# Rounding to fp4 in the last stage of a transformer layer: the power of two from two bits, the clamp inside the addition, and the scales of x and h together

## The chip, the cores and the metric

The kernel runs on one core of one Trainium2 chip. The core has a matrix engine (TensorE, PE in the rows), a vector engine (VectorE, DVE), a scalar engine (ScalarE, ACT), a general engine (GpSimd, POOL) and a queue for transfers (SyncE, SP). They run side by side and wait for each other on semaphores. The metric is the device time of one execution in microseconds (us); lower is better. The profile is one execution on the chip, and its times count from the start of its span.

## The reference

The layer takes x of 4 x 2048 tokens with 256 channels. In short:

```python
x = layernorm(x + attention(x))        # 16 heads of 16, rotary positions, softmax
x = layernorm(x + ffn(x))

def fp4_quant_dequant(x):              # blocks of 16 along the last dimension
    scale = max(max(abs(block)) / 6, 1e-12)
    xn = block / scale                 # so |xn| <= 6
    idx = searchsorted([0.25, 0.75, 1.25, 1.75, 2.5, 3.5, 5.0], abs(xn))
    return [0, .5, 1, 1.5, 2, 3, 4, 6][idx] * sign(xn) * scale

def fp4_linear(x, w): return fp4_quant_dequant(x) @ fp4_quant_dequant(w).T
def ffn(x):                            # 256 -> 704 -> 256
    h = silu(fp4_linear(x, w_gate)) * fp4_linear(x, w_up)
    return fp4_linear(h, w_down)
```

The grid has steps of 0.5 below 2, of 1 from 2 to 4 and of 2 above 4. The step follows from the power of two p = 1, 2 or 4 at or below |xn| (1 for everything smaller). Adding p * 1.5 * 2^22 to xn in float32 and subtracting it again rounds xn to the grid.

## The kernel before

Three stages follow each other: projections and rotary positions (to about 310 us), attention (to about 3115 us), and the last stage, which this document is about (about 3115 us to the end). The last stage goes over 64 tiles of 128 tokens. On each engine one list of functions says what is done in step s, each entry with a lag: an entry (6, f) runs f on tile s - 6. `run_steps` writes this list out for the first and last steps, and between them makes a loop (`Fori`) whose body holds four steps, with semaphore values computed from a register; `run_straight` writes all steps out with constants. The order within a step is the order of the list, and every engine works its instructions strictly in that order.

What a step s does on each engine, in order, with the tile in brackets:

- **VectorE**: every fourth step the small arithmetic of the inverse deviations, `inverse_std` (L988 to L993), in front; then `residual2` [s-10] (L1007, L1009), `residual1` [s-2] (L1000, L1002); every fourth step `variance` (L961 to L969); then `quantise_xh`: x of tile s-6 and h of tile s-8 in one hand-written interleaving of eight operations each (k = 1 to 8, lines L853 to L868); then `silu_up` [s-7] (L1037).
- **GpSimd**: `normalise` [s-1] (L1124, L1125), `round_x` [s-6] and `round_h` [s-8] in two halves, each a subtraction (L1130) and a multiplication by the scale (L1132). In the order of time, `normalise` stands ahead of `round_x` of the same step, that is, right behind `round_h` of the step before.
- **TensorE**: transposes of x [s-7] (L657), `proj` [s-2] (L649), `gate_up` [s-7] (L679), transposes of h [s-9] (L670), `down` [s-9] (L689).
- **ScalarE**: copy of the transposed x [s-7] (L803), `norm2` [s-14] (L793), `norm1` [s-6] (L787), the store, every fourth step a square root (L827) with two table loads, `silu` [s-7] (L820), copies of the transposed h [s-9] (L810, L813).

Three buffer waits matter. `residual2` of tile n waits for `norm2` of tile n-4, whose row it overwrites (`o_done`). `residual1` of tile n waits for `norm1` of tile n-4 (`x1_done`). `norm1` waits for `residual2` of the same step (`y2_done`). The eight operations of the rounding on VectorE are, for x (256 columns, 16 blocks) and for h (704 columns, 44 blocks): k=1 largest magnitude of each block, k=2 the inverse scale's base, k=3 the scale, k=4 reciprocal, k=5 values times the inverse, k=6 the exponent bits (an AND with 0x7F800000), k=7 the power of two clamped from below at 1 and times 1.5 * 2^22, k=8 the sum. k=6 and k=7 read one tensor and constants; k=5 and k=8 read two tensors in SBUF.

Of the kernel before, what the change touches and what calls it, by code (L numbers as in the profile page):

```python
# [22 lines left out]
I32 = mybir.dt.int32  # L23
ALU = mybir.AluOpType
ACT = mybir.ActivationFunctionType
AX = mybir.AxisListType

P = 128
# [32 lines left out]
ROUND = 1.5 * 2.0 ** 22  # L61
EXPONENT = 0x7F800000
TILES_S = KT * CHUNKS
PAIRS = TILES_S // 2
# [58 lines left out]
def run_steps(eng, total, stages):  # L123


    longest = max(lag for lag, _ in stages)

    first = -(-(longest + UNROLL) // UNROLL) * UNROLL
    last = total // UNROLL * UNROLL

    def straight(s):
        for lag, fn in stages:
            if 0 <= s - lag < total:
                fn(At(0, s - lag))

    if last - first < UNROLL:
        first = last = total + longest
    for s in range(first):
        straight(s)
    if last > first:  # L140
        with eng.Fori(0, (last - first) // UNROLL) as register:
            i = Turn(eng, register)
            for u in range(UNROLL):
                for lag, fn in stages:
                    fn(At(i, first + u - lag))
        for s in range(last, total + longest):
            straight(s)

# [32 lines left out]
def layer_kernel(nc, x, xT, sinT, cosT, w_qk, w_v, b_qk, b_v, w_proj, b_proj, w_gate, w_up, w_down, eye, out):  # L181
    nc.disable_value_cache = True
    ctx = ExitStack()
    with ctx:
# [3 lines left out]
        def sem(name):  # L188
            return ctx.enter_context(nc.semaphore(name))
# [96 lines left out]
        std, rstd, shift, ln_t, ln_d, sums, var = (take(8) for _ in range(7))  # L286
        x_am, x_sc, x_inv = ([take(C // BLK) for _ in range(2)] for _ in range(3))
        h_am, h_sc, h_inv = ([take(FF // BLK) for _ in range(2)] for _ in range(3))
        hh_r = [v_all[:, i * FF:(i + 1) * FF] for i in range(4)]
# [33 lines left out]
        var_step, std_done, ln_step, x1_done = (sem(n) for n in ("var_step", "std_done", "ln_step", "x1_done"))  # L323
        xq_step, xr_step, xh_done, xhT_psum, xhT_out = (sem(n) for n in ("xq_step", "xr_step", "xh_done", "xhT_psum", "xhT_out"))
        gu_psum, e_done, h_done = (sem(n) for n in ("gu_psum", "e_done", "h_done"))
# [13 lines left out]
        def _(sp):  # L339
# [121 lines left out]
            def load_tile(b, q, c):  # L461

                if not isinstance(q, int):
# [15 lines left out]
            for p in range(4):  # L479
                sp.wait_ge(inv_out[p], 16 * G // 4)  # L480
            with sp.Fori(1, KT // 4) as q:
                for c in range(4):
                    load_tile(0, q, c)
            with sp.Fori(1, B) as b:
                with sp.Fori(0, KT // 4) as q:
                    for c in range(4):
                        load_tile(b, q, c)


        @block.tensor  # L490
        def _(pe):
# [200 lines left out]

            run_steps(pe, TILES, [(7, xT_tile), (2, proj), (7, gate_up), (9, hT_tile), (9, down)])


        @block.scalar
        def _(act):
# [125 lines left out]
            def deviation(n, alone):  # L823
# [4 lines left out]

            run_steps(act, TILES, [
                (7, xT_out), (14, norm2), (6, norm1), (14, store_out),  # L830
# [6 lines left out]
        def _(dve):  # L837
            def quantise(jobs):
# [4 lines left out]
                def bc(a, blocks):  # L843
                    return a.unsqueeze(2).broadcast_to([P, blocks, BLK])
                order = [(0, k) for k in range(1, 9)]
                if len(jobs) > 1:
                    order = [(int(o[0] == "b"), int(o[1])) for o in "a1 b1 a2 a3 b2 a4 b3 a5 b4 a6 b5 a7 a8 b6 b7 b8".split()]
                for j, k in order:
                    for x, xn, m, am, sc, inv, step, at, blocks in jobs[j:j + 1]:
                        if k > 1:  # L850
# [159 lines left out]

            def job_x(n):
                p = n.u % 2
# [3 lines left out]
                return (x1_r[n.u], xh_r[n.u], xm_r[p], x_am[p], x_sc[p], x_inv[p], xq_step, lambda k: n.times(8, k), C // BLK)  # L1016

            def job_h(n):
                p = n.u % 2
                wait_after(dve, hq_done, n.times(2, -2))  # L1020
                dve.wait_ge(h_done, n.times(2, 2))
                return (hh_r[n.u], hh_r[n.u], hm_r[p], h_am[p], h_sc[p], h_inv[p], hq_step, lambda k: n.times(8, k), FF // BLK)

            def quantise_xh(n):

                quantise([job_x(n)] + ([job_h(n.back(2))] if n.c >= 2 else []))

            def quantise_last_h(n):
                if n.static(TILES - 2) or n.static(TILES - 1):
                    quantise([job_h(n)])  # L1030

            def silu_up(n):
# [6 lines left out]

            run_steps(dve, TILES, [  # L1040
                (3, lambda n: inverse_std(n, False)), (11, lambda n: inverse_std(n, True)),
# [5 lines left out]
        def _(pool):  # L1047
# [79 lines left out]
            def rounded(t, m, sc, step, at, done, blocks):  # L1127

                v = t.rearrange("p (b e) -> p b e", e=BLK)
                nc.gpsimd.tensor_tensor(t, t, m, ALU.subtract).then_inc(step, 1)  # L1130
                pool.wait_ge(step, at)
                nc.gpsimd.tensor_tensor(v, v, sc.unsqueeze(2).broadcast_to([P, blocks, BLK]), ALU.mult).then_inc(done, 1)  # L1132

            def round_x(n):
                pool.wait_ge(xq_step, n.times(8, 8))
                rounded(xh_r[n.u], xm_r[n.u % 2], x_sc[n.u % 2], xr_step, n.times(1, 1), xh_done, C // BLK)

            def round_h(n):
                p, nb = n.u % 2, FH // BLK
                for hf in range(2):  # L1140
                    cols = slice(hf * FH, (hf + 1) * FH)
                    pool.wait_ge(hq_step, n.times(8, 8))
                    rounded(hh_r[n.u][:, cols], hm_r[p][:, cols], h_sc[p][:, hf * nb:(hf + 1) * nb], hr_step,
                            n.times(2, hf + 1), hq_done, nb)

            run_steps(pool, TILES, [(1, normalise), (6, round_x), (8, round_h)])


# [38 lines left out]
```

## Time and profile before

| | us |
|---|---|
| median of 3 runs (lowest to highest) | 3878.07 (3875.76 to 3878.23) |
| the profiled execution's own time | 3876.52 |
| its span | 3874.7 |
| TensorE busy over the span | 3617.4 (93%) |
| VectorE busy over the span | 3350.5 (86%) |
| GpSimd busy over the span | 712.0 (18%) |

Some 1.8 us of the execution lie outside the span. The times in the rows are start and duration; `DVE`, `POOL`, `ACT` are the engines, `L868` is a line of the kernel before, `x1` the number of instructions in a row, and the square bracket at the end of a row is the time that the engine stood idle before it, with whom it waited for.

### The profile page before, as it was taken

The numbers are of one execution on the slowest core, as the hardware profiler recorded it, in microseconds if no ns is written. First come the engines' busy times: TensorE is split into PE (matmuls) and PEld (weight loads), VectorE is DVE, ScalarE is ACT, GpSimd is POOL, SyncE is SP. The second block draws the span as 40 slices with busy tenths as digits, with TensorE's granted clock in tenths as the row PEclk, the third lists the DMA queues.
The fourth block names the chain that finished last, engine by engine and source line by source line (L and its number), as shares of the span: only waits on it lengthen the run. The fifth ranks groups of instructions, "written<-read, shape, count | busy, mean of one in ns | idle before, by whom it ended". The sixth has DMA issues, their size and how long they took to land.

```text
span 3874.7 us, 56176 instructions
## 1 busy us (share of the span) xinstructions
PE 3617.4 (93%) x19560; PEld 1556.6 (40%) x19560; DVE 3350.5 (86%) x3879; ACT 2527.9 (65%) x4870; POOL 712.0 (18%) x883
## 2 busy tenths in 40 slices
PE   7769999999999999999999999999999978888887
PEld 4433333333333333333333333333333346656665
DVE  7998888888888888888888888888888379999997
ACT  4334777777777777777777777777777723333333
POOL 6870000000000000000000000000000045555554
PEclk9887999999999999999999999999999989999999
DMA  5441111111111111111111111111111111111110
GB/s 153 161 167 53 44 39 38 44 45 40 37 43 45 41 37 42 46 42 37 40 47 42 38 39 48 42 38 38 46 44 39 29 50 45 43 47 45 47 37 20
DMA packets 121153, 195.55 MB, mean 50 GB/s; under 512 B 28640, under 2 KB 83040, under 8 KB 108640
## 3 DMA queue, kind: packets, MB, share of 16 engines
q1 hardware_dynamic: 111712, 184.16, 14.2%
q10 hardware_dynamic: 9216, 8.39, 0.6%
q8 instruction: 140, 2.29, 0.2%
q14 instruction: 85, 0.70, 0.1%
HBM read 139.55 MB, written 51.38 MB: 49 GB/s over the span
## 4 chain that ended last, share of the span: by engine, by line
PE 70%; issue 10%; POOL 8%; DVE 7%; ACT 3%; DMA 1%; POOLq 0%; SPq 0%; ACTq 0%; DVEq 0%
PE ps L563 28%; PE ps L605 26%; PE ps L594 14%; POOL v_all L1130 2%; ACT arena L772 2%; DVE arena L904 2%; DVE arena L909 1%; POOL arena L1130 1%; POOL arena L1132 1%; POOL arena L1124 1%; POOL arena L1125 1%; DVE arena L927 1%; PE ps L679 1%; DVE arena L897 1%; POOL arena L1065 1%
## 5 line engine op out<-in xcount | busy, mean ns | idle before, releaser
L927 DVE TENSOR_REDUCE arena<-ps 128x1 f32<-128x1024 f32 x2048 | 2412.7, 1220 | 332.8 <-PE ps L563 326.5
L772 ACT ACTIVATE arena<-ps 128x512 f32<-128x512 f32 x4096 | 2122.0, 604 | 622.5 <-PE ps L594 622.4
L594 PE MATMUL ps<-qst,kst 51*128 51x512 f32 x4096 | 1529.7, 453 | 31.1 <-ACT arena L772 7.7
L563 PE MATMUL ps<-kst,qst 48*128 48x512 f32 x4096 | 1284.4, 433 | 27.5 <-DMA qst<-qk_parts 23.2
L605 PE MATMUL ps<-arena 128*32 128x512 f32 x8192 | 1092.5, 605 | 2.4
L563 PEld LDWEIGHTS ps<-kst,qst 48*128 48x128 f32 x4096 | 622.8, 187 | 1090.0 <-DVE arena L927 942.9
L594 PEld LDWEIGHTS ps<-qst,kst 51*128 51x128 f32 x4096 | 677.3, 184 | 493.6 <-ACT arena L772 491.5
L1107 POOL TENSOR_TENSOR arena<-arena,ones 128x16 bf16<-128x16 f32 x64 | 14.2, 222 | 2640.5 <-DVE arena L932 2640.5
L605 PEld LDWEIGHTS ps<-arena 128*32 128x32 f32 x8192 | 163.0, 108 | 245.3 <-ACT arena L772 148.9
L689 PE MATMUL ps<-wdT,arena 128*128 128x256 f32 (+1 forms) x768 | 191.0, 400 | 36.1 <-ACT arena L810 36.1
L679 PE MATMUL ps<-wgT,arena 128*128 128x352 f32 x512 | 202.3, 478 | 3.5 <-DVE v_all L1037 2.5
L679 PE MATMUL ps<-wuT,arena 128*128 128x352 f32 x512 | 198.6, 470 | 0.0
L803 ACT ACTIVATE arena<-ps 128x256 f32<-128x256 f32 x64 | 24.5, 383 | 247.3 <-PE ps L657 247.3
L689 PEld LDWEIGHTS ps<-wdT,arena 128*128 128x128 f32 (+1 forms) x768 | 146.0, 197 | 69.9 <-ACT arena L810 42.0
L820 ACT ACTIVATE v_all<-ps 128x352 f32<-128x352 f32 x128 | 56.6, 462 | 122.8 <-PE ps L679 121.4
L1130 POOL TENSOR_TENSOR v_all<-v_all 128x352 f32<-128x352 f32 x128 | 119.3, 932 | 60.4 <-DVE v_all L868 60.4
L536 PE MATMUL ps<-arena 128*128 128x512 f32 x256 | 117.5, 613 | 12.6 <-DMA arena<-in_b_qk 9.4
L679 PEld LDWEIGHTS ps<-wuT,arena 128*128 128x128 f32 x512 | 100.5, 196 | 57.7 <-issue 6.2
L679 PEld LDWEIGHTS ps<-wgT,arena 128*128 128x128 f32 x512 | 97.7, 198 | 56.9 <-ACT arena L803 6.8
L735 ACT ACTIVATE arena<-ps,arena 128x512 f32<-128x512 f32 x64 | 41.2, 700 | 116.2 <-DMA qk_parts<-arena 105.2
L543 PE MATMUL ps<-arena 128*128 128x256 f32 x256 | 69.5, 432 | 40.5 <-ACT v_all L726 40.5
L1130 POOL TENSOR_TENSOR arena<-arena 128x256 f32<-128x256 f32 x64 | 59.7, 932 | 254.0 <-DVE arena L868 254.0
(101 smaller groups left out, 2282.7 us busy)
## 6 DMA issues: line engine op xcount, KB each, us to landing
qk_parts<-arena SPq DMA_DIRECT2D x32, 1024.0 KB, 7.4
kst<-qk_parts SPq DMA_DIRECT2D x128, 256.0 KB
qst<-qk_parts SPq DMA_DIRECT2D x128, 256.0 KB
kst<-qk_parts SPq DMA_DIRECT2D x128, 128.0 KB
qst<-qk_parts SPq DMA_DIRECT2D x128, 128.0 KB
att<-arena SPq DMA_DIRECT2D x256, 34.0 KB
arena<-in_xT SPq DMA_DIRECT2D x16, 512.0 KB, 8.2
arena<-att SPq DMA_DIRECT2D x128, 64.0 KB
```

What stands on the lines that cost most here:

```text
L536: mm = nc.tensor.matmul(ps[:, m, :], wqk[:, c, m * P:(m + 1) * P], xt[p][:, c], start=(c == 0), stop=(c == CT - 1))
L543: mm = nc.tensor.matmul(ps[:, 4 + v, t * C:(t + 1) * C], xt[p][:, c, (2 * v + t) * P:(2 * v + t + 1) * P], wv[:, c], start=(c == 0), stop= ...
L563: mm = nc.tensor.matmul(ps[:, i % S_BANKS, :], q[SROW:SROW + STACK, qt * P:(qt + 1) * P], k[SROW:SROW + STACK, kc * CHUNK:(kc + 1) * CHUNK ...
L594: nc.tensor.matmul(ps[:, t_bank(t_place(g.c, i)), :], kst[g.u % 2][0:ROWS, kb * P:(kb + 1) * P], qst[g.u % 2][0:ROWS, qb * CHUNK:(qb + 1) ...
L605: mm = nc.tensor.matmul(ps[32 * qb:32 * qb + 32, O_BANK, :], vs[g.u % 2][:, kb, :], pt[kb % 2][:, qb * CHUNK:(qb + 1) * CHUNK], start=(kb ...
L679: mm = nc.tensor.matmul(ps[:, bank, 0:FH], xhT_r[n.u % 2][:, ct], w[:, ct, hf * FH:(hf + 1) * FH], start=(ct == 0), stop=(ct == CT - 1))
L689: mm = nc.tensor.matmul(ps[:, 7, 0:C], hT_r[n.u % 2][0:nf, j], wdT[0:nf, k], start=(j == 0), stop=(j == 5))
L772: nc.scalar.activation(pt[kb % 2][:, qb * CHUNK:(qb + 1) * CHUNK], ps[:, t_bank(t_place(g.c, i)), :], ACT.Exp).then_inc(p_ready, 1)
L820: nc.scalar.activation(e_r[n.u % 2][:, hf * FH:(hf + 1) * FH], ps[:, 2 + 2 * hf, 0:FH], ACT.Silu).then_inc(e_done, 1)
L904: nc.vector.tensor_tensor(x, x, rot[p], ALU.add).then_inc(qr_done, 1)
L927: nc.vector.tensor_reduce(mx[g.u % 2][:, i // 2, i % 2:i % 2 + 1], ps[:, bank:bank + 2, :].rearrange("p b t -> p (b t)"), AX.X, ALU.max).t ...
L1130: nc.gpsimd.tensor_tensor(t, t, m, ALU.subtract).then_inc(step, 1)
```

## The change

In the last stage only. The rounding takes the power of two and its product with 1.5 * 2^22 in one integer operation: an AND with 0x40800000 leaves the exponent's top and lowest bits, and an XOR with 0x0B400000 makes from them exactly 4 or 2 times 1.5 * 2^22 where |xn| is 4 or 2 and more, and a tiny number otherwise. The clamp (a maximum with 1.5 * 2^22) is then taken inside the addition, as a three-input operation (`scalar_tensor_tensor`, max and add). The tile m therefore no longer holds the clamped number that GpSimd subtracts, so GpSimd takes the same maximum on its own copy first: one `tensor_scalar` more in front of each of its three subtractions per tile. The base of the inverse, the scale and the reciprocal are computed once for the 16 blocks of x and the 44 of h side by side (60 numbers). Loops become straight code on all five engines (`run_steps` goes; SP's `Fori` loops over the tile loads too).

```diff
+POWER_BITS, TO_ROUND = 0x40800000, 0x0B400000
...
+            def scales(p, cols, turn):
+                nc.vector.tensor_scalar(q_inv[p][:, cols], q_am[p][:, cols], BELOW / 6.0, 1e-12 * BELOW, ALU.mult, ALU.max
+                                        ).then_inc(q_small, 1)
+                nc.vector.tensor_scalar(q_sc[p][:, cols], q_am[p][:, cols], 1.0 / 6.0, 1e-12, ALU.mult, ALU.max
+                                        ).then_inc(q_small, 1)
+                dve.wait_ge(q_small, turn.times(3, 1))
+                nc.vector.reciprocal(q_inv[p][:, cols], q_inv[p][:, cols]).then_inc(q_small, 1)
+                dve.wait_ge(q_small, turn.times(3, 3))
...
+            def powers_x(n):
+                dve.wait_ge(x_scaled, n.times(1, 1))
+                nc.vector.tensor_scalar(xm_r[n.u % 2].bitcast(I32), xh_r[n.u].bitcast(I32), POWER_BITS, TO_ROUND,
+                                        ALU.bitwise_and, ALU.bitwise_xor).then_inc(x_power, 1)
+            def round_x(n):
+                dve.wait_ge(x_power, n.times(1, 1))
+                nc.vector.scalar_tensor_tensor(out=xh_r[n.u], in0=xm_r[n.u % 2], scalar=ROUND, in1=xh_r[n.u],
+                                               op0=ALU.max, op1=ALU.add).then_inc(xq_step, 1)
...
             def quantise_xh(n):
-                quantise([job_x(n)] + ([job_h(n.back(2))] if n.c >= 2 else []))
+                p, h = n.u % 2, n.back(2)
+                largest_x(n)
...
+                largest_h(h)
+                dve.wait_ge(q_max, n.times(2, 0))
+                scales(p, slice(0, HB.stop), n)
+                scale_x(n)
+                scale_h(h)
+                powers_x(n)
+                round_x(n)
+                powers_h(h)
+                round_h(h)
...
             def rounded(t, m, sc, step, at, done, blocks):
                 v = t.rearrange("p (b e) -> p b e", e=BLK)
+                nc.gpsimd.tensor_scalar(m, m, ROUND, None, ALU.max).then_inc(step, 1)
+                pool.wait_ge(step, at[0])
                 nc.gpsimd.tensor_tensor(t, t, m, ALU.subtract).then_inc(step, 1)
-                pool.wait_ge(step, at)
+                pool.wait_ge(step, at[1])
                 nc.gpsimd.tensor_tensor(v, v, sc.unsqueeze(2).broadcast_to([P, blocks, BLK]), ALU.mult).then_inc(done, 1)
...
-            run_steps(pool, TILES, [(1, normalise), (6, round_x), (8, round_h)])
+            run_straight(TILES, [(1, normalise), (6, round_x), (8, round_h)])
```

## Rows read from the trace of the kernel before

**Rows 1.** Busy time of the engines in a stretch of 100 us of the last stage:

```profile
core 0: us, PE busy (x) PEld busy (x) DVE busy (x) ACT busy (x) POOL busy (x), PEclk, DMA share, GB/s
3400.00:3500.00 100.00, 85.38 (x353) 60.16 (x352) 92.15 (x218) 32.40 (x66) 56.57 (x70) 0.98 0.17 47
```

**Rows 2.** VectorE in order of time, one step without small arithmetic:

```profile
3394.87 0.43 DVE L868 TENSOR_TENSOR arena<-arena 128x256 f32<-128x256 f32 x1
...
3395.77 0.93 DVE L866 TENSOR_SCALAR v_all<-v_all 128x704 f32<-128x704 f32 x1
3396.73 1.19 DVE L868 TENSOR_TENSOR v_all<-v_all 128x704 f32<-128x704 f32 x1
...
3398.85 0.42 DVE L1007 TENSOR_TENSOR arena<-ps,arena 128x256 f32<-128x256 f32 x1
...
3400.89 0.42 DVE L853 TENSOR_REDUCE arena<-arena 128x16 f32<-128x256 f32 x1
...
3402.25 0.71 DVE L855 TENSOR_SCALAR arena<-arena 128x44 f32<-128x44 f32 x1
...
3405.10 0.42 DVE L868 TENSOR_TENSOR arena<-arena 128x256 f32<-128x256 f32 x1
```

**Rows 3.** GpSimd in order of time in the same step:

```profile
3395.38 0.94 POOL L1130 TENSOR_TENSOR arena<-arena 128x256 f32<-128x256 f32 x1 [5.54 <-DVE arena L868]
3396.39 0.78 POOL L1132 TENSOR_TENSOR arena<-arena 128x256 f32<-128x256 f32 x1
...
3401.51 0.72 POOL L1124 TENSOR_TENSOR arena<-arena 128x256 f32<-128x256 f32 x1
```

**Rows 4.** ScalarE in order of time in the same step:

```profile
3398.23 0.59 ACT L793 ACTIVATE arena<-arena 128x256 f32<-128x256 f32 x1
```

**Rows 5.** VectorE, the rounding of a step in which GpSimd was done:

```profile
3437.09 0.42 DVE L853 TENSOR_REDUCE arena<-arena 128x16 f32<-128x256 f32 x1
...
3438.37 0.18 DVE L855 TENSOR_SCALAR arena<-arena 128x44 f32<-128x44 f32 x1
...
3439.09 0.42 DVE L859 RECIPROCAL arena<-arena 128x44 f32<-128x44 f32 x1
...
3439.57 0.88 DVE L861 TENSOR_TENSOR v_all<-v_all,arena 128x704 f32<-128x704 f32 x1
...
3440.68 0.43 DVE L868 TENSOR_TENSOR arena<-arena 128x256 f32<-128x256 f32 x1
```

**Rows 6.** VectorE, the two steps with small arithmetic:

```profile
3415.35 0.43 DVE L868 TENSOR_TENSOR arena<-arena 128x256 f32<-128x256 f32 x1
...
3427.58 0.43 DVE L868 TENSOR_TENSOR arena<-arena 128x256 f32<-128x256 f32 x1
...
3431.43 0.18 DVE L988 RECIPROCAL arena<-arena 128x8 f32<-128x8 f32 x1
...
3435.05 0.42 DVE L1007 TENSOR_TENSOR arena<-ps,arena 128x256 f32<-128x256 f32 x1 [0.75 <-ACT arena L793]
```

**Rows 7.** GpSimd's groups by line and shape, whole span (count, busy us, mean ns):

```profile
L1130 POOL TENSOR_TENSOR v_all<-v_all 128x352 f32<-128x352 f32 x128 | 119.3, 932 | 60.4 <-DVE v_all L868 60.4
L1132 POOL TENSOR_TENSOR v_all<-v_all,arena 128x352 f32<-128x352 f32 x128 | 100.8, 788 | 10.0
...
L1100 POOL COPY arena<-v_all 128x256 f32<-128x256 f32 x64 | 25.4, 396 | 0.0
...
L1091 POOL MEMSET arena<- 128x240 f32 x2 | 0.6, 302 | 0.0
```

**Rows 8.** First stage, in order of time: VectorE beside GpSimd, then GpSimd alone:

```profile
110.68 2.28 DVE L897 TENSOR_TENSOR arena<-arena 128x2048 f32<-128x2048 f32 x1
...
110.84 6.51 POOL L1071 TENSOR_TENSOR arena<-arena 128x2048 f32<-128x2048 f32 x1 [1.16 <-DVE arena L909]
...
274.11 4.51 POOL L1071 TENSOR_TENSOR arena<-arena 128x2048 f32<-128x2048 f32 x1 [3.49 <-DVE arena L909]
```

**Rows 9.** VectorE, the same operation four steps apart in steps written out straight:

```profile
3189.73 0.41 DVE L1007 TENSOR_TENSOR arena<-ps,arena 128x256 f32<-128x256 f32 x1
...
3235.30 0.42 DVE L1007 TENSOR_TENSOR arena<-ps,arena 128x256 f32<-128x256 f32 x1
```

More of the change, by code:

```diff
@@ L120, in run_straight @@
                 fn(At(0, s - lag))
[L123 to L147, printed above, removed]
 def t_place(g, i):
@@ L286, in layer_kernel @@
         std, rstd, shift, ln_t, ln_d, sums, var = (take(8) for _ in range(7))
-        x_am, x_sc, x_inv = ([take(C // BLK) for _ in range(2)] for _ in range(3))
-        h_am, h_sc, h_inv = ([take(FF // BLK) for _ in range(2)] for _ in range(3))
+        XB, HB = slice(0, C // BLK), slice(C // BLK, C // BLK + FF // BLK)
+        q_am, q_sc, q_inv = ([take(HB.stop) for _ in range(2)] for _ in range(3))
         hh_r = [v_all[:, i * FF:(i + 1) * FF] for i in range(4)]
@@ L480, in _ @@
                 sp.wait_ge(inv_out[p], 16 * G // 4)
[L481 to L487, printed above, removed]
+            for tile in range(4, TILES):
+                load_tile(tile // KT, tile % KT // 4, tile % 4)
         @block.tensor
@@ L844, in bc @@
                     return a.unsqueeze(2).broadcast_to([P, blocks, BLK])
[L845 to L849, printed above, removed]
+                for k in range(1, 9):
+                    for x, xn, m, am, sc, inv, step, at, blocks in jobs:
                         if k > 1:
@@ L1009, in residual2, with blocks, over, largest_x @@
                 nc.vector.bn_stats(bn[:, 4 + n.u], y2_r[n.u]).then_inc(y2_step, 1)
-            def job_x(n):
-                p = n.u % 2
+            def blocks(a):
+                return a.rearrange("p (b e) -> p b e", e=BLK)
+            def over(small, cols):
+                return small[:, cols].unsqueeze(2).broadcast_to([P, cols.stop - cols.start, BLK])
+            def scales(p, cols, turn):
[6 more added lines that the diff above has]
+                dve.wait_ge(q_small, turn.times(3, 3))
+            def largest_x(n):
                 dve.wait_ge(x1_done, n.times(1, 1))
@@ L1015, in job_x, with largest_h @@
                 wait_after(dve, xh_done, n.times(1, -1))
-                return (x1_r[n.u], xh_r[n.u], xm_r[p], x_am[p], x_sc[p], x_inv[p], xq_step, lambda k: n.times(8, k), C // BLK)
-            def job_h(n):
-                p = n.u % 2
+                nc.vector.tensor_reduce(q_am[n.u % 2][:, XB], blocks(x1_r[n.u]), AX.X, ALU.max, apply_absolute_value=True
+                                        ).then_inc(q_max, 1)
+            def largest_h(n):
                 wait_after(dve, hq_done, n.times(2, -2))
@@ L1021, in job_h, with scale_x @@
                 dve.wait_ge(h_done, n.times(2, 2))
-                return (hh_r[n.u], hh_r[n.u], hm_r[p], h_am[p], h_sc[p], h_inv[p], hq_step, lambda k: n.times(8, k), FF // BLK)
-            def quantise_xh(n):
-                quantise([job_x(n)] + ([job_h(n.back(2))] if n.c >= 2 else []))
+                nc.vector.tensor_reduce(q_am[n.u % 2][:, HB], blocks(hh_r[n.u]), AX.X, ALU.max, apply_absolute_value=True
+                                        ).then_inc(q_max, 1)
+            def scale_x(n):
+                nc.vector.tensor_tensor(blocks(xh_r[n.u]), blocks(x1_r[n.u]), over(q_inv[n.u % 2], XB), ALU.mult
+                                        ).then_inc(x_scaled, 1)
@@ new lines, in scale_h @@
+            def scale_h(n):
+                nc.vector.tensor_tensor(blocks(hh_r[n.u]), blocks(hh_r[n.u]), over(q_inv[n.u % 2], HB), ALU.mult
+                                        ).then_inc(h_scaled, 1)
+            def powers_x(n):
+                dve.wait_ge(x_scaled, n.times(1, 1))
+                nc.vector.tensor_scalar(xm_r[n.u % 2].bitcast(I32), xh_r[n.u].bitcast(I32), POWER_BITS, TO_ROUND,
+                                        ALU.bitwise_and, ALU.bitwise_xor).then_inc(x_power, 1)
@@ new lines, in round_h @@
+            def round_h(n):
+                dve.wait_ge(h_power, n.times(1, 1))
+                nc.vector.scalar_tensor_tensor(out=hh_r[n.u], in0=hm_r[n.u % 2], scalar=ROUND, in1=hh_r[n.u],
+                                               op0=ALU.max, op1=ALU.add).then_inc(hq_step, 1)
+            def quantise_xh(n):
+                p, h = n.u % 2, n.back(2)
+                largest_x(n)
+                if n.c < 2:
+                    dve.wait_ge(q_max, n.c + 1)
+                    scales(p, XB, n)
+                    scale_x(n)
+                    powers_x(n)
+                    round_x(n)
+                    return
+                largest_h(h)
+                dve.wait_ge(q_max, n.times(2, 0))
+                scales(p, slice(0, HB.stop), n)
+                scale_x(n)
+                scale_h(h)
+                powers_x(n)
+                round_x(n)
+                powers_h(h)
+                round_h(h)
```

33 lines of the change are left out of this document (22 added, 11 removed).

## The prediction

> **What bounds the kernel now.** I read the busy time by stretches first. In the last stage VectorE is busy 92% of the time, GpSimd 57%, and TensorE runs at a granted clock of 0.98 [rows 1]. So VectorE seems the bound, and an edit that takes work off it seems a gain. The engines' instructions in order of time show more. Call t = 0 the start of the sum of x (k=8) on VectorE. From there to the next one a plain step takes 3405.10 - 3394.87 = 10.23 us [rows 2], and it is a ring through four engines. GpSimd subtracts and multiplies x until 3396.39 + 0.78 = 3397.17 (t = 2.30) [rows 3]; TensorE transposes, ScalarE copies and then runs `norm2` until 3398.82 [rows 4]; `residual2` starts on VectorE at 3398.85, the first block maximum at 3400.89, and the next k=8 at 3405.10 [rows 2]. In pieces: 2.30 + 1.68 + 2.04 + 4.21. VectorE's other work in between (h and `silu_up`) ends just as `residual2` may start, so VectorE and the ring are tied. Four steps are a period: two plain ones, one with the variances (12.23), one with the inverse deviations (3440.68 - 3427.58 = 13.10) [rows 6], 45.81 in all, and 16 periods in the stage.
>
> The second thing to see is that VectorE and GpSimd stand in each other's way. GpSimd's operation over 2048 takes 4.51 alone and 6.51 when VectorE's two-input one of 2.28 began just before it [rows 8]: it waited nearly all of it. VectorE's sum of h takes 1.19 [rows 2] where an operation of that size takes 0.88 [rows 5], because it started 0.44 before GpSimd's multiplication ended; a scale operation on 44 numbers takes 0.71 under GpSimd's `normalise` [rows 2, 3] and 0.18 without it [rows 5]. So I reckon with a lock: of such operations one runs and the other waits to its end. The Trainium skill (SBUF — State Buffer, "Who interferes with whom") says the same of the port pair that the two engines share, and that a VectorE operation with one SBUF input outside the fast modes is free of it; by that rule the reductions, `residual2` and `silu_up` never wait, and the trace agrees.
>
> **The change, part by part.** *Off VectorE:* k=7 of h (0.93 [rows 2]), k=7 of x and three small operations. The sum stays a two-tensor operation; as the kernel before has no three-input one of this size I take the price of the old sum, 0.88 free of waits. The AND with XOR costs as the AND. *On the ring, the rounding of x:* from the first maximum to the scale operation that needs both maxima 3438.37 - 3437.09 = 1.28; that operation and the wait for it 0.22; the reciprocal of 60 numbers 0.52 (0.42 for 44 [rows 5], 0.57 in proportion) and its wait 0.04; scaling x until scaling h starts 0.34; from there to k=8 now 3440.68 - 3439.57 = 1.11 [rows 5], less 0.05. That is 3.46, against 3.59 now in a step free of GpSimd and 4.21 in a plain one. *On GpSimd:* three clamps per tile. The trace has no such operation. Its nearest row is the copy, also one tensor in and one out: 0.40 for 256 columns, so about 0.50 for 352; below it lies the memset of 240 (0.30, so 0.40), above it the two-input operations, 0.72 for 256 and 0.93 for 352 [rows 3, 7]. I take the copy and keep both ends. Each clamp also adds a wait of 0.08.
>
> The Trainium skill (GPSIMD Engine Reference, section 3.1) gives 1.03 cycles per element at 1.2 GHz for a loop body of up to two operations, 0.22 us for 256 columns plus the dispatch, and its standing rule is to leave elementwise work to the vector engine. By that figure, an estimate, the clamp lies between memset and copy, and the sum below would come out some 10 us lower; no row here shows the clamp itself.
>
> *A plain step put together.* On VectorE the powers of h run from t = 0.34 to 0.86. GpSimd's clamp of x is issued at 0.51, waits for them as its subtraction does now (0.94 instead of 0.72 [rows 3]), and ends at 1.12. The sum of h waits for it and runs to 1.86. The subtraction waits for that sum and ends at 2.44, the multiplication at 3.14 instead of 2.30: 0.84 late. This is what is late next. Straight code gives back about 0.15 of the 1.68 behind it: in the steps already written out straight a period is 3235.30 - 3189.73 = 45.57 [rows 9] instead of 45.81. So `residual2` starts at 4.67 and the first maximum at 6.71; VectorE stands idle for 2 us before `residual2`, so the time saved on h buys nothing there. The scale operation would be ready at 7.99. But GpSimd goes straight from x to h: its two halves take twice 0.50 + 0.08 + 0.93 + 0.08 + 0.75 from t = 3.10, to 7.78, and the first `normalise` operation then holds the lock to 8.51. The scale operation waits for it, the reciprocal starts at 8.6, and k=8 comes 1.96 later, at 10.6. Plain step: 10.6 instead of 10.23, that is +0.35, twice in a period.
>
> *The step with the variances.* Six small operations follow `residual1`; from 6.83 on, four of them each meet one GpSimd operation (ends 6.95, 7.82, 8.51, 9.20). The first maximum comes at 9.27, k=8 at 12.75: +0.5. *The step with the inverse deviations.* Here VectorE itself leads to `norm2`, and h's saving counts: the first small operation starts at 2.65 instead of 3431.43 - 3427.58 = 3.85 [rows 6]. The seven meet two to three GpSimd operations and end at 4.95 to 5.55; `residual2` starts at 5.7 to 6.3 instead of 7.47, and k=8 comes at 11.55 to 11.8, so 11.7: -1.4.
>
> *Sum:* 0.35 + 0.35 + 0.5 - 1.4 = -0.2 us per period, times 16 = -3 us. The other edits go with it: GpSimd is then busy some 8.2 of 10.6 us and keeps up; TensorE, which needs about 9.75 us a step, only gets more idle time; SP's loads are issued on the same condition (`y_done` three tiles back) and stay ahead of `normalise`. Straight code as such has no cost that the attention stage, straight already, shows. 3876.5 - 3 = 3873.5 for an execution like the profiled one, which lies 1.5 under the median; on the median, 3875.
>
> **The rivals.** *A cheap clamp (memset's price, 0.30 and 0.40).* Everything behind it comes earlier: plain steps 10.3, the variance step 12.55, the inverse step 11.4; -1.25 per period, 3858. For it: one input, one operation. *The clamp at a two-input price (0.73, 0.93).* The multiplication of x ends at 3.47, GpSimd's halves at 8.8, and `normalise` then also blocks the scaling of h: plain steps 11.35, the others 13.4 and 11.9, +2.2 per period, 3913. This is the one that ends on the other side, slower; the clamp decides it, and the point at which it passes no change is near 0.42 for 256 columns. *The addition does not hold GpSimd up* (only the fast modes would lock): the subtraction ends at 1.84, plain steps fall to 9.95, and the period by 2.5: 3838. Against it stand rows 8, where a plain two-input operation did. *VectorE was the bound after all:* it loses about 1.6 us a step, but TensorE's 9.75 us and the ring both stand in front of that; at best as the case before.
>
> **How the numbers follow.** The forecast case (3862 to 3888) has 0.42, the cheap clamp 0.22, the dear one 0.20, no lock by the addition 0.07, and 0.09 goes to lost races for the lock on VectorE's small operations, a few tenths each, slower by 10 to 20 us. A difference under 0.2%, 7.8 us, can't be told from none. Within the forecast case I give a quarter to faster, half to the same, a quarter to slower; so faster is 0.10 + 0.20 + 0.07 = 0.37, the same 0.21 and 0.08 from the edges of the rivals = 0.29, slower the rest, 0.34. The range runs from between the cheap clamp and the lock-free case to short of the dear clamp: 3850 to 3908.
>
> **What would show it.** The clamp's own duration for 256 and 352 columns. GpSimd's multiplication of x ending at t = 3.1, its busy share rising from 57% to about 75%. A 2 us gap on VectorE before `residual2` in plain steps, put down to `norm2`, and a scale operation on 60 numbers that takes 0.6 to 0.7 instead of 0.2. Steps of 10.6, 10.6, 12.7 and 11.7. The forecast is wrong if the clamp is not near 0.4, if the three-input operation is slower than 0.88, or if the operations win or lose the lock in another order than I laid out.

## The result, and the profile after

| | before | changed | |
|---|---|---|---|
| median, us (15 runs each, same chip) | 3875.76 | 3890.89 | ratio 1.0059 [1.0044, 1.0075] |
| profiled execution, us | 3876.52 | 3889.72 | its span 3874.7 and 3887.7, +13.0 |
| VectorE busy, us | 3350.5 | 3283.4 | -67.1 |
| GpSimd busy, us | 712.0 | 927.1 | +215.1 |

The kernel became slower: by 15.1 us between the medians (0.4%), by 0.6% in the ratio, whose interval does not hold 1. Five of the changed kernel's 15 runs lie at 3910 to 3920 (last section), none of the kernel before's; the other ten have a median of 3889.9, still 14 us above before. VectorE was relieved as planned, by 67 us, and GpSimd took on three times as much. The forecast was no change, 3875 us; the measured median is 16 us above it.

First the stretch of 100 us of the last stage, busy time of the engines (answers to [rows 1]):

```profile
core 0: us, PE busy (x) PEld busy (x) DVE busy (x) ACT busy (x) POOL busy (x), PEclk, DMA share, GB/s
3400.00:3500.00 100.00, 81.24 (x339) 57.12 (x340) 79.54 (x170) 33.15 (x66) 84.99 (x95) 1.00 0.17 44
```

GpSimd went from 57 to 85%, VectorE from 92 to 80%, TensorE from 85 to 81%. No engine is full, and the step became longer: a sign that they wait for each other. The groups by line and shape show what one clamp takes (answers to [rows 7]; columns: count, busy us, mean ns, idle time before):

```profile
L1167 POOL TENSOR_SCALAR v_all<-v_all 128x352 f32<-128x352 f32 x128 | 139.0, 1086 | 3.7 <-DVE v_all L1036 3.7
...
L1167 POOL TENSOR_SCALAR arena<-arena 128x256 f32<-128x256 f32 x64 | 66.9, 1045 | 93.5 <-DVE arena L1031 93.5
```

A clamp of 352 columns takes 1.09 us: more than the subtraction of two tensors of that size, 0.93 [rows 7], and more than twice what I took from the copy. The 1.05 of a clamp of x (256 columns) contains a wait for VectorE. At the start of the stage, where VectorE has no h to work on yet, it takes 0.85:

```profile
3126.92 0.85 POOL L1167 TENSOR_SCALAR arena<-arena 128x256 f32<-128x256 f32 x1 [3.14 <-DVE arena L1031]
```

Together, 139.0 + 66.9 = 205.9 us of GpSimd's 215.1 are clamps.

VectorE in order of time, one plain step of the changed kernel (answers to [rows 2]):

```profile
3398.36 0.43 DVE L1031 SCALAR_TENSOR_TENSOR arena<-arena 128x256 f32<-128x256 f32 x1
...
3399.26 0.96 DVE L1036 SCALAR_TENSOR_TENSOR v_all<-v_all 128x704 f32<-128x704 f32 x1
...
3403.01 0.42 DVE L978 TENSOR_TENSOR arena<-ps,arena 128x256 f32<-128x256 f32 x1 [1.92 <-ACT arena L767]
...
3405.06 0.40 DVE L1002 TENSOR_REDUCE arena<-arena 128x16 f32<-128x256 f32 x1
...
3406.29 0.27 DVE L990 TENSOR_SCALAR arena<-arena 128x60 f32<-128x60 f32 x1
...
3407.58 1.42 DVE L1016 TENSOR_TENSOR v_all<-v_all,arena 128x704 f32<-128x704 f32 x1
3408.91 0.81 DVE L1021 TENSOR_SCALAR arena<-arena 128x256 int32<-128x256 int32 x1
3409.76 0.42 DVE L1031 SCALAR_TENSOR_TENSOR arena<-arena 128x256 f32<-128x256 f32 x1
```

GpSimd in the same step (answers to [rows 3]):

```profile
3398.88 1.05 POOL L1167 TENSOR_SCALAR arena<-arena 128x256 f32<-128x256 f32 x1 [1.50 <-DVE arena L1031]
3400.01 0.80 POOL L1169 TENSOR_TENSOR arena<-arena 128x256 f32<-128x256 f32 x1
...
3401.47 1.09 POOL L1167 TENSOR_SCALAR v_all<-v_all 128x352 f32<-128x352 f32 x1
...
3406.59 0.79 POOL L1171 TENSOR_TENSOR v_all<-v_all,arena 128x352 f32<-128x352 f32 x1
3407.33 0.91 POOL L1161 TENSOR_TENSOR arena<-arena 128x256 f32<-128x256 f32 x1
3408.21 1.37 POOL L1162 TENSOR_TENSOR arena<-arena,bp_bc 128x256 f32<-128x256 f32 x1
```

Read the two side by side. The step takes 3409.76 - 3398.36 = 11.40 us instead of 10.23. The 1.92 us gap on VectorE before `residual2` (L978) is the one forecast. New is the end of the step. GpSimd finishes h only at 3407.38, and `normalise` (L1161, L1162) then lies exactly over the scaling of h (L1016) and the powers of x (L1021). These take 1.42 and 0.81, where 0.88 and 0.28 are their times with nothing in the way (they are seen in the first experiment). 0.54 + 0.53 = 1.07 us are lost there, on the way to the next sum of x.

The four steps of a period take 11.40, 11.40, 12.36 and 11.66, in all 46.82.

### The profile page after: what moved, and what is told of

The parts are those of the page before. It is cut to its first block, busy times and chain, and to the rows that moved or that the text cites. A ratio compares the mean times of both kernels' runs of the same rounds, so it can differ in the third digit from the quotient of the medians.

```text
span 3887.7 us, 52715 instructions
## 1 busy us (share of the span) xinstructions
PE 3599.6 (93%) x19560; PEld 1541.5 (40%) x19560; DVE 3283.4 (84%) x3565; ACT 2533.0 (65%) x4870; POOL 927.1 (24%) x1075
## 4 chain that ended last, share of the span: by engine, by line
PE 69%; DVE 16%; POOL 5%; ACT 4%; issue 3%; DMA 1%; SPq 0%; DVEq 0%; ACTq 0%; POOLq 0%
PE ps L537 28%; PE ps L579 26%; PE ps L568 14%; ACT arena L746 2%; DVE v_all L1016 2%; DVE arena L875 2%; POOL arena L1167 1%; DVE arena L1008 1%; DVE arena L880 1%; POOL arena L1169 1%; ACT arena L761 1%; ACT arena L767 1%; POOL arena L1171 1%; DVE arena L1012 1%; DVE arena L995 1%
## 5 line engine op out<-in xcount | busy, mean ns | idle before, releaser
L1167 POOL TENSOR_SCALAR v_all<-v_all 128x352 f32<-128x352 f32 x128 | 139.0, 1086 | 3.7 <-DVE v_all L1036 3.7
L631 PE MATMUL ps<-ident,arena 128*128 128x128 f32 x128 | 28.4, 304 | 105.7 <-POOL arena L1171 105.7
```

What stands on the lines that cost most here:

```text
L1167: nc.gpsimd.tensor_scalar(m, m, ROUND, None, ALU.max).then_inc(step, 1)
```

## The experiments

Each kernel was compared with the kernel before on the same chip; that one's median was 3877.26 for e1 to e4, 3879.04 for e5 to e8 and 3876.76 for e9 to e12. Steps of a period are given from one `residual2` or one sum of x to the next.

**e1: the changed kernel without GpSimd's clamps (4 runs).** It leaves the clamp out, so numbers under 2 come out wrong and only its time is read.

```diff
-                nc.gpsimd.tensor_scalar(m, m, ROUND, None, ALU.max).then_inc(step, 1)
-                pool.wait_ge(step, at[0])
```

> The changed kernel without GpSimd's clamp; GpSimd then subtracts the unclamped number, so values whose magnitude is under 2 come out wrong and the time alone is read. Theory A (the clamps' time on GpSimd makes the kernel slower: they hold up x and push GpSimd's later work into VectorE's scaling): plain steps fall from 11.40 to about TensorE's 9.75 us, the period from 46.8 to 42.8, and the time to about 3830 (3815 to 3845). Theory B (the joined scales or the straight code are what costs): it stays within 10 us of the changed kernel, about 3885.

Measured 3833.16, ratio 0.9881 [0.9867, 0.9896]. Against the kernel before this is -44.1 us, and against the changed kernel, each by its own comparison, -59.2: the clamps are the whole loss and more. VectorE in order of time, in e1:

```profile
3403.58 0.88 DVE L1016 TENSOR_TENSOR v_all<-v_all,arena 128x704 f32<-128x704 f32 x1
3404.38 0.28 DVE L1021 TENSOR_SCALAR arena<-arena 128x256 int32<-128x256 int32 x1
3404.70 0.43 DVE L1031 SCALAR_TENSOR_TENSOR arena<-arena 128x256 f32<-128x256 f32 x1
...
3405.59 1.30 DVE L1036 SCALAR_TENSOR_TENSOR v_all<-v_all 128x704 f32<-128x704 f32 x1
...
3408.87 0.42 DVE L978 TENSOR_TENSOR arena<-ps,arena 128x256 f32<-128x256 f32 x1 [1.12 <-ACT arena L767]
```

GpSimd, whose `normalise` now ends at 3401.01, is out of the way, and the step is 9.71 (from 3399.16 to 3408.87 on L978). The three-input sum of h takes 1.30 here because it waits for GpSimd's subtraction of x (the first row below), and it then holds up the multiplication (the second, 1.15 instead of 0.62); in the changed kernel, beside a clamp, the sum took 0.96. TensorE is busy for 9.45 us of this step, so a further gain elsewhere could hardly shorten it; the 9.75 us a step that the prediction gave TensorE stood in no row, and this comes near it.

```profile
3405.20 0.94 POOL L1167 TENSOR_TENSOR arena<-arena 128x256 f32<-128x256 f32 x1 [4.20 <-DVE arena L1031]
3406.22 1.15 POOL L1169 TENSOR_TENSOR arena<-arena 128x256 f32<-128x256 f32 x1
```

**e2: the kernel before with its loops written out straight, and nothing else.**

```diff
-            run_steps(pool, TILES, [(1, normalise), (6, round_x), (8, round_h)])
+            run_straight(TILES, [(1, normalise), (6, round_x), (8, round_h)])
```

(and so on the other four engines.)

> The kernel before with all loops of the last stage written out straight, and nothing else. Theory A: 3873, 3 us less than before (the four-step period goes from 45.81 to about 45.6). Theory B: slower than before by 5 us or more, from the straight code's fetching or its longer waits.

Measured 3871.71, 1.0000 [0.9984, 1.0017]: the median is 5.6 lower, the ratio cannot be told from 1. In the last stage straight code gives a little. But 3 of the 12 runs are 21 to 30 us longer than the middle of the others, and they bring the ratio back to 1; the last section returns to this.

**e3: e2 with the scales of x and h together, and the rounding as before.** VectorE's order is then: both largest magnitudes, base, scale and reciprocal of 60 numbers, scaling x, scaling h, k=6 to 8 of x, k=6 to 8 of h.

```diff
+                nc.vector.tensor_scalar(q_inv[p][:, cols], q_am[p][:, cols], BELOW / 6.0, 1e-12 * BELOW, ALU.mult, ALU.max
+                                        ).then_inc(q_small, 1)
...
+                nc.vector.reciprocal(q_inv[p][:, cols], q_inv[p][:, cols]).then_inc(q_small, 1)
```

> The changed kernel with the rounding of before (exponent bits, then clamp and product on VectorE, no clamp on GpSimd): straight code and joined scales alone. Theory A: x's ring loses up to 0.7 us in plain steps; plain steps 9.5 to 10.1, period about 43.6, time about 3840 (3830 to 3860). Theory B: at or above 3876, because the scales of x now wait for the reduction of h as well.

Measured 3885.75, 1.0040 [1.0020, 1.0060]. I expected 3840. The three small operations saved do not pay: against e2 (+14.0 us between the medians; the mean period of the last stage is 46.42 instead of 45.72) this part makes the kernel slower. VectorE in order of time, e2:

```profile
3407.92 0.40 DVE L848 TENSOR_REDUCE arena<-arena 128x16 f32<-128x256 f32 x1
...
3409.03 0.39 DVE L850 TENSOR_SCALAR arena<-arena 128x16 f32<-128x16 f32 x1
...
3409.50 0.24 DVE L854 RECIPROCAL arena<-arena 128x16 f32<-128x16 f32 x1
...
3411.72 0.43 DVE L863 TENSOR_TENSOR arena<-arena 128x256 f32<-128x256 f32 x1
```

and e3:

```profile
3408.69 0.40 DVE L1002 TENSOR_REDUCE arena<-arena 128x16 f32<-128x256 f32 x1
...
3409.92 0.30 DVE L990 TENSOR_SCALAR arena<-arena 128x60 f32<-128x60 f32 x1
3410.14 0.77 DVE L992 TENSOR_SCALAR arena<-arena 128x60 f32<-128x60 f32 x1
3410.83 0.52 DVE L995 RECIPROCAL arena<-arena 128x60 f32<-128x60 f32 x1
...
3413.17 0.43 DVE L1035 TENSOR_TENSOR arena<-arena 128x256 f32<-128x256 f32 x1
```

From the first maximum to the sum of x it takes 3.80 in e2 (4.13 in the step before it) and 4.48 in e3. Without any meeting with GpSimd it is 3.59 (e2, 3420.07 to 3423.66) and 3.81 (e3, 3399.00 to 3402.81). Joined, the six small operations become three and take 0.79 instead of 0.87. But the first of them now waits for the end of h's maximum too (0.91 after that one's start instead of 0.79), and k=6 of x has k=7 of x right behind it, which needs its result and starts 0.33 later; in e2 the scaling of h stands between them and starts after 0.14. The scaling of h lies in front of the sum of x in both. And where one scale operation meets `normalise`, x and h both wait for it (0.77 instead of 0.19). Not all of this reaches the step: e3's plain steps are 10.36, e2's 10.24 and 10.39. Joining and the order that came with it were not tried apart.

**e4: the changed kernel with `normalise` between x and h on GpSimd.**

```diff
-            run_straight(TILES, [(1, normalise), (6, round_x), (8, round_h)])
+            run_straight(TILES, [(6, round_x), (0, normalise), (8, round_h)])
```

> The changed kernel with GpSimd's normalise put between the rounding of x and that of h, one tile earlier (lag 0). Theory A1 (it is the two normalise operations that block VectorE's scaling of h and powers of x, 0.54 us each in a plain step): the blocked 1.1 us shrinks, time 3870 to 3880. Theory A2 (GpSimd is so full that some other two-input operation takes their place in VectorE's way): within 6 us of the changed kernel, 3884 to 3896.

Measured 3886.11, 1.0051 [1.0030, 1.0072]: 8.9 us above the kernel before, where the changed kernel is 15.1 above. `normalise` is out of the critical place, but in the plain steps h's operations have come into it. VectorE, then GpSimd, in e4:

```profile
3407.49 1.05 DVE L1012 TENSOR_TENSOR arena<-arena 128x256 f32<-128x256 f32 x1
3408.47 1.47 DVE L1016 TENSOR_TENSOR v_all<-v_all,arena 128x704 f32<-128x704 f32 x1
```

```profile
3407.34 0.93 POOL L1169 TENSOR_TENSOR v_all<-v_all 128x352 f32<-128x352 f32 x1
3408.34 0.85 POOL L1171 TENSOR_TENSOR v_all<-v_all,arena 128x352 f32<-128x352 f32 x1
```

Now the scaling of x (1.05) and of h (1.47) wait. The plain step stays at 11.4; the 6 us gained come from the step with the variances, 11.73 instead of 12.36. Which operation of GpSimd blocks is a matter of order. That one does goes, I argue, with how full it is.

**e5 and e6: the clamp of x alone, and the clamps of h alone.** e5 leaves out the two clamps of h, e6 that of x, so in each some small numbers come out wrong.

> The changed kernel with GpSimd's clamp of x kept and both clamps of h left out (h's small values come out wrong, the time alone is read). Theory R (the clamp costs because it stands on the ring of x): as slow as the changed kernel, 3885 to 3892. Theory F (it costs because GpSimd fills up and its normalise reaches into VectorE's scaling): close to the kernel without clamps, 3835 to 3845. My own sum, with both at work: plain steps 10.3, period 44.4, time 3852.

> The changed kernel with the clamps of h kept and that of x left out (x's small values come out wrong, the time alone is read). Theory R: close to the kernel without clamps, 3835 to 3845. Theory F: as slow as the changed kernel, 3880 to 3892. My own sum: plain steps 10.8, period 44.8, time 3858.

e5 measured 3854.89, 0.9945 [0.9917, 0.9972], plain steps of 10.18 (my sum: 3852). e6 measured 3868.52, 0.9967 [0.9939, 0.9995], plain steps of 10.92 (my sum: 3858). Against e1's -44.1 us (each by its own kernel before) the clamp of x adds 20.0, those of h 33.6, and all three 59.2. Both ways are at work, and the traces price each. The clamp of x sits on the ring through the four engines: in e5 the multiplication of x ends 3.14 us after the start of the sum of x, in e1 2.67, and that is the 0.47 by which the step is longer (10.18 and 9.71). The clamps of h are not on the ring at all and cost more, because they keep GpSimd busy until `normalise` falls on the next rounding: in e6 x is ready at 2.67 as in e1, but from the first maximum to the sum of x it takes 4.68 instead of 3.48, again the whole difference of the step (10.92 and 9.71). The changed kernel has both, 3.15 and 4.70, and 9.71 + 0.48 + 1.22 is its 11.40 to 0.01. GpSimd's groups in e6 show the meeting, in the second operation of `normalise`:

```profile
L1162 POOL TENSOR_TENSOR arena<-arena,bp_bc 128x256 f32<-128x256 f32 x60 | 59.3, 988 | 0.0
```

In e5 the same operation takes 729 ns: no meeting. (Both are means over the last stage.)

**e7: the changed kernel with separate scales, and e8: e7 with GpSimd's clamps taken from another place.** e7 returns to the hand-written interleaving of before, without k=7. e8 writes the clamped number to a tile of its own, so the clamp waits only for the powers and runs beside VectorE's sum.

```diff
-                c = m
-                pool.wait_ge(ready, after[1])
+                c = v_all[:, 8 * FF + clamped[0]:8 * FF + clamped[0] + blocks * BLK]
+                pool.wait_ge(ready, after[0])
```

> The changed kernel with the scales of x and of h computed apart again, in the interleaving of before (the addition with its clamp, the two bits, GpSimd's clamps and the straight code stay). If the joined scales cost the 14 us that lie between the straight kernel and the one with straight code and joined scales: 3876, as fast as before. Rival: with GpSimd as full as it is, what the shorter path of x gains is lost to waits for GpSimd, and it stays at 3885 to 3892.

> As e7_separate, and GpSimd clamps into a tile of its own as soon as the powers are there, beside VectorE's addition instead of behind it. Theory R: x comes 0.4 us earlier on the ring in three of four steps, 15 to 20 us less than e7_separate, about 3860. Theory F: GpSimd's work is the same and merely starts 0.4 us earlier, at most 5 us less than e7_separate.

e7 measured 3893.03, 1.0029 [1.0009, 1.0049]; e8 3891.75, 1.0030 [1.0008, 1.0052]. Neither gives anything over the changed kernel. Separate scales gave 14 us in e2 against e3, where GpSimd was 57% busy, and nothing here. In both the second theory of the expectation held, e7's within 1 us. In e8 the clamp of x starts early and finds VectorE's operations in its way, the scaling of h above all: GpSimd in order of time, e8:

```profile
3400.96 1.41 POOL L1140 TENSOR_SCALAR v_all<-arena 128x256 f32<-128x256 f32 x1 [1.23 <-DVE arena L863]
...
3403.40 1.15 POOL L1145 TENSOR_TENSOR arena<-arena 128x256 f32<-128x256 f32 x1
```

1.41 instead of 1.05 (0.85 with nothing in the way), and the multiplication 1.15 instead of 0.62. Measured from the start of the sum of x, x is ready at 2.97 (3404.55 - 3401.58) and not at 3.15, but that sum itself starts later.

**e9 to e12: can the kernel before be beaten without clamps on GpSimd?** e9 is e2 with `normalise` between x and h (the edit of e4). e10 is e2 with `silu_up` moved ahead of k=6 of h, so that h's sum no longer meets GpSimd's work on x. e11 is both. e12 is e3 with the edit of e4.

```diff
-            def quantise(jobs):
+            def quantise(jobs, between=None):
...
+                    if between and (j, k) == (1, 6):
+                        between()
...
+                    quantise([job_x(n), job_h(n.back(2))], lambda: silu_up(n.back(1)))
```

> The straight kernel of before's rounding (as e2_straight), with GpSimd's normalise between the rounding of x and that of h, one tile earlier. In a plain step of e2_straight two small scale operations wait for normalise, 0.2 and 0.55 us. With room on GpSimd (57% busy, not 85%) moving normalise should remove most of it: plain steps 9.9 to 10.1 instead of 10.39, time 3858. Rival (something always stands in the way, as in e4_norm_mid): within 5 us of e2_straight, 3867 to 3877.

> The straight kernel of before's rounding, with VectorE's silu_up (it reads PSUM and one SBUF tensor) moved between the sum of x and the last three operations on h. GpSimd then rounds x while VectorE works on something that does not take the lock: x is ready 0.2 to 0.4 us earlier, and the product and the sum of h lose their waits of 0.4 and 0.3. Plain steps 9.75 to 9.9, time 3840 to 3850. Rival: silu is not ready that early and VectorE waits for ScalarE instead; 3872 or slower.

> Both of the two moves at once. TensorE's 9.75 us then bounds the plain steps; period about 43.2, time about 3832 to 3842. Rival: the two remove the same waits, no better than e10_silu_first.

> Joined scales and straight code with before's rounding (as e3_scales), with normalise moved as in e9. If the joined scales were slow only because their two operations wait for normalise (0.11 and 0.58 in a plain step of e3_scales): 3855, as e9 or better. If they are slow because x now waits for the maxima and the reciprocal of h too: 10 us or more above e9_straight_norm.

| | median, us | ratio | mean of 11 periods, us (e2: 45.72) |
|---|---|---|---|
| e9 (12 runs) | 3869.19 | 1.0003 [0.9981, 1.0026] | 45.48 |
| e10 (12 runs) | 3863.46 | 0.9987 [0.9966, 1.0007] | 45.18 |
| e11 (5 runs) | 3893.78 | 1.0045 [1.0032, 1.0058] | 45.40 |
| e12 (9 runs) | 3908.50 | 1.0063 [1.0041, 1.0085] | 46.72 |

e10 has the lowest median of the complete kernels, 13.3 under before, but its interval holds 1: in 4 of its 12 runs, 5 of e9's 12, 5 of e12's 9 and all of e11's, the time is some 30 us longer, in the profiled ones at the end of attention (last section). What e10 does in the last stage is seen on VectorE:

```profile
3443.58 0.89 DVE L865 TENSOR_TENSOR v_all<-v_all 128x704 f32<-128x704 f32 x1
3444.66 0.42 DVE L1004 TENSOR_TENSOR arena<-ps,arena 128x256 f32<-128x256 f32 x1 [0.19 <-ACT arena L788]
```

`silu_up` (L1039) reads one tensor in SBUF and runs while GpSimd works on x; the sum of h (L865) comes after and takes 0.89 instead of 1.19 [rows 2]. From one `residual2` to the next, before has 15.71, 9.61, 10.25, 10.24 (45.81), and e10 14.89, 9.33, 10.41, 10.40 (45.03), both without dips of the clock. The gain lies in the long interval, which holds the variances and the inverse deviations and in which VectorE itself leads to `norm2`; the other three are 30.14 instead of 30.10 in sum. 0.8 x 16 = 13 us, what was measured. I had expected 3840 to 3850, from plain steps that get shorter. e9's plain steps did (10.05), but its step with the inverse deviations grew (13.36 instead of 13.09 in e2); expected 3858, it stayed near e2, as its rival said. e11, expected at 3832 to 3842, has no shorter period than e10: its rival held. e12, the joined scales once more, is slower than e9 even in its four quickest runs (3877.98 to 3887.43, against 3863.57 to 3869.20 in e9's seven), which repeats what e3 showed. With `normalise` moved away the joined scales still lose more than 10 us, so the meeting with it was not their only cost.

## Why the prediction was wrong, point by point

**The step that failed is the price of the clamp.** It read: "I take the copy and keep both ends", that is 0.40 for 256 columns and 0.50 for 352. Measured: 0.85 for 256 and 1.09 for 352, and 1.05 for x in a plain step, where 0.20 are the wait for VectorE's powers of h. Even my upper end, the price of an operation with two inputs, was too low, by 0.12 and 0.16. "One tensor in and one out" made the copy look like the nearest row. It was not: copy and clamp both read one tensor, and the clamp takes twice the time. The Trainium skill (GPSIMD Engine Reference, section 3.1) gives 1.03 cycles per element at 1.2 GHz for a loop body of up to two operations, an estimate of 0.30 us for 352 columns, and about 2.6 cycles, an estimate of 0.76 us, for one with two inputs, plus the dispatch. The subtraction (0.93) agrees with the second; the clamp (1.09) lies above both, though it has one input. The rule of that section of the Trainium skill, to leave elementwise work to the vector engine, spoke against the change and held: with the clamps on GpSimd the kernel is 59 us slower than without (e1).

**The mechanism of the rival with the dear clamp was right**, chance 0.20: the halves of h end late (t = 3407.38 - 3398.36 = 9.02, there 8.8), `normalise` blocks the scaling of h, plain steps of 11.35 (measured 11.40), inverse step 11.9 (11.66). Only its step with the variances was too dear, 13.4 against 12.36, and so its time, 3913. That rival priced the clamp at 0.73 and 0.93, less than it takes. That the kernel came out at 3891, inside the range I gave, owes something to luck: the clamp was dearer than any case I had, and the next error worked against it.

**The assumption that the clamp holds the lock like a two-input operation was wrong.** I had the sum of h wait for the clamp of x. It did not wait: 0.96 from 3399.26, while the clamp ran from 3398.88 to 3399.93. And I had four small operations of the variances each meet one GpSimd operation. VectorE, and GpSimd below it, in that step of the changed kernel:

```profile
3427.98 0.17 DVE L932 TENSOR_TENSOR arena<-arena 128x8 f32<-128x8 f32 x1
3428.07 0.17 DVE L933 TENSOR_TENSOR arena<-arena 128x8 f32<-128x8 f32 x1
3428.15 0.16 DVE L934 TENSOR_TENSOR arena<-arena 128x8 f32<-128x8 f32 x1
3428.23 0.16 DVE L936 TENSOR_TENSOR arena<-arena 128x8 f32<-128x8 f32 x1
...
3428.51 0.82 DVE L940 SCALAR_TENSOR_TENSOR arena<-arena 128x8 f32<-128x8 f32 x1
```

```profile
3427.20 1.08 POOL L1167 TENSOR_SCALAR v_all<-v_all 128x352 f32<-128x352 f32 x1
3428.37 0.93 POOL L1169 TENSOR_TENSOR v_all<-v_all 128x352 f32<-128x352 f32 x1
```

Four operations with two inputs pass under one clamp without a wait, and the one that meets the subtraction takes 0.82. This error hid the first at one place: the multiplication of x ends at t = 3.15, forecast 3.14, for the dearer clamp and the missing wait cancel, which is luck. So the ring up to the first maximum came out as laid down (`residual2` at t = 4.65, forecast 4.67; first maximum 6.70, forecast 6.71; gap 1.92, forecast 2), and all the loss is behind it.

**The order at the end of the step was wrong in consequence.** Forecast: the first `normalise` operation holds up the scale operation, 0.6 to 0.7. Measured: that operation took 0.27, GpSimd was still in h's second half, and `normalise` fell two operations later, on L1016 and L1021, where it cost 1.07 us instead of 0.5.

**The sum.** Plain steps 11.40 instead of 10.6, twice: +1.6 a period; variances 12.36 instead of 12.7: -0.3; inverse deviations 11.66 as forecast. The period is 46.82 and not 45.6, +1.2, times 16 = +19.5. From this go 3 us: before, every second period has a plain step of 10.61 and not 10.24, which I left out of the 45.81 (mean 46.0), and the changed kernel has none. 3873.5 + 19.5 - 3 = 3890 for the profiled execution; it took 3889.72. That close an agreement is in part chance: one period of the kernel before took 47.39, for 46.15 in the mean, and the steps at both ends of the stage aren't in the sum.

**Parts of the change, as the runs price them** (differences of median against the kernel before of the same chip): straight code -5.6, joined scales +14.0 (e3 less e2), two bits and the clamp inside the sum on VectorE -52.6 (e1 less e3), GpSimd's clamps +59.2. They add up to the +15.1 by construction, since each is the difference of neighbouring kernels. I had the chain from the first maximum to the sum of x right, 3.46 (measured 3.48 in e1, 3404.70 - 3401.22), but not where its gain over 3.59 comes from: with k=7 of x it is 3.81 (e3), so the gain is all k=7's, and the joined scales in their order cost 0.22. That VectorE "was the bound after all" was put aside too quickly. In e3's plain steps VectorE has no idle time in front of `residual2`; with k=7 and the clamps gone too, in e1, it waits there for 1.12 us, and the kernel is 44 us faster than before. Between e3 and e1 the plain step falls from 10.36 to 9.71: the chain by 1.00 (0.33 for k=7 of x, 0.67 for the meetings with `normalise` that are gone), while `residual2` starts 0.33 later behind the sum of x (4.17 instead of 3.84): the sum of h now meets GpSimd's subtraction of x, and x is ready at 2.67 instead of 2.30.

**What stays open.** The clamp's price and the lock work together: e6 loses its time in waits for the lock, which come up because the clamps take GpSimd so long. What the kernel would do with a clamp at the price of a copy, which is what the forecast assumed, could not be tried.

## What to carry to other kernels

An operation moved to another engine is priced by that same operation on that engine, or measured alone first; the nearest row by the number of tensors was off by a factor of two. An engine far from full can still set the time: ask when its last operation of a step ends, and which operation of the other engine is then on the path. And count, before joining two small computations to save instructions, what the urgent one must now wait for: here the joining saved 0.08 us of small operations and, with the order that came with it, cost 0.31 in waits.

## What the runs showed of the hardware

**A clamp on GpSimd frees the lock early.** A maximum with a constant over 352 columns of float32 takes 1.09 us, more than a subtraction of two tensors (0.93). VectorE's two-input operations run beside it, except at its beginning: in the changed kernel one (L961) starts 0.09 us after a clamp (GpSimd, 3436.64) and takes 0.41 instead of 0.17:

```profile
3436.73 0.41 DVE L961 TENSOR_TENSOR arena<-arena 128x8 f32<-128x8 f32 x1
3437.17 0.17 DVE L962 TENSOR_SCALAR arena<-arena 128x8 f32<-128x8 f32 x1
```

In all 19 meetings of this kind in the changed kernel's last stage, started 0.05 to 0.30 us after a clamp of 352 columns, the wait ends 0.33 us after the clamp's start; none of the small operations started later waits (L963, 0.74 after it, takes 0.17).

The Trainium skill (SBUF — State Buffer, "Who interferes with whom") says that whoever issues first has the shared pair for the whole instruction. For GpSimd's subtractions, multiplications and `normalise` the traces agree, for its clamp they do not.

**A faster step meets TensorE's clock.** The granted clock in stretches of the last stage, first before, then e1:

```profile
3345.00:3350.00 5.00, 2.86 (x12) 2.19 (x12) 4.87 (x16) 0.84 (x3) 0.81 (x1) 1.00 0.20 55
3350.00:3355.00 5.00, 3.79 (x10) 2.69 (x11) 4.56 (x9) 1.47 (x3) 3.94 (x6) 0.67 0.16 51
```

```profile
3425.00:3430.00 5.00, 3.33 (x17) 2.46 (x15) 4.86 (x10) 1.14 (x3) 1.51 (x2) 1.00 0.33 80
3430.00:3435.00 5.00, 4.37 (x12) 2.94 (x13) 3.45 (x9) 1.47 (x3) 4.84 (x7) 0.67 0.08 26
```

In these the clock stands at 1.2 GHz for part of the second stretch and then at 2.4 GHz again; TensorE was busy 2.86 and 3.33 of 5 us in the one before. That alone doesn't tell when it falls: before, 3395 to 3400 has TensorE busy for 2.60 us, and the next stretch shows 1.00. A dip costs 0.37 us in every second period before (10.61 instead of 10.24), and 1.5 us in most periods of e1 (11.25 instead of 9.71). The changed kernel shows 1.00 from 3150 to 3865, with TensorE busy only 81%. Why the more idle kernel is spared was not tried.

**A long stretch at half the clock in some executions.** At the end of attention, in code that no kernel here changes, before and e10 differ like this in their profiled executions:

```profile
3060.00:3080.00 20.00, 17.69 (x90) 6.11 (x93) 0.25 (x1) 16.18 (x32) 0.00 (x0) 1.00 0.34 87
```

```profile
3060.00:3080.00 20.00, 20.00 (x60) 6.36 (x52) 0.25 (x1) 10.24 (x21) 0.00 (x0) 0.50 0.22 51
```

The mean times of the two kinds of matmul there go from 444 and 605 ns to 708 and 1061, and the execution takes some 30 us more. TensorE was busy without a break meanwhile. Other executions of the same kernel don't have it: runs of e10 lie at 3861 to 3866 or at 3893 to 3896. The traces show it in e9, e10 and e11. In the other kernels only the time and the mean clock of a run point to it: the changed kernel's five long runs were granted 0.966 to 0.971, its others 0.976 to 0.978. Counting such runs (18 us or more above the middle of the others, and all of e11's), the kernel before has 4 of 106, and the kernels in straight code 41 of 137: the changed one 5 of 15, e2, which differs from before in nothing else, 3 of 12, e1 none of 4. So straight code may well raise their number; what starts them was not tried. The medians above contain such runs, and this widens the intervals, those of e9 to e12 most.
